# Decoder layer on one core: both V parts behind the scores of step 1, later feed-forward transposes and statistics, and one tile for B and C in the mixer

## The reference, cut to what matters

```python
# 1, mixer: u, B, C go through a causal convolution of 4 taps and a silu
zgate, u, Bc, Cc, dt = jnp.split(proj, [DIN, 2 * DIN, 2 * DIN + N_, 2 * DIN + 2 * N_], axis=-1)
Bc = Bc * jax.lax.rsqrt(jnp.sum(Bc * Bc, -1, keepdims=True) + 1e-06)
Cc = Cc * jax.lax.rsqrt(jnp.sum(Cc * Cc, -1, keepdims=True) + 1e-06)
z = (z + d * (Bu - A * y)) / (1.0 + d * d * A)      # per token, state of 16 per head
y = y + d * z                                        # out = y . C_t, then an MLP
# 2, attention: 16 heads of 64, one K and V for all heads, context of 375 tokens
attn = jax.nn.softmax(jnp.einsum('bhid,bjd->bhij', q, k) + mask[:, None, :, :], axis=-1)
out = jnp.einsum('bhij,bjd->bhid', attn, v)
out = out.transpose(0, 2, 1, 3).reshape(b, n, INNER) @ Wout + jax.nn.silu(gate) * val @ W2
# 3, feed-forward with both operands of the second product rounded to 8 bits
out = jnp.einsum('bsh,dh->bsd', hq, wq) + bq
```

## Time and profile before

| | us |
|---|---|
| three executions | 1742.54, 1746.35, 1747.15 |
| median | 1746.35 |
| the profiled execution | 1751.45 |
| its span, first to last instruction | 1749.6 |
| PE busy | 1604.0 (92%) |
| DVE busy | 1275.5 (73%) |
| ACT busy | 983.7 (56%) |
| POOL busy | 542.9 (31%) |

### The profile page before, as it was taken

One profiled execution on the slowest core, in us unless ns is written; L12 is line 12 of the kernel. 1 busy time (PEld: TensorE's weight loads), 2 busy tenths in 40 slices (PEclk: granted clock), 3 DMA queues, 4 the chain that ended last, 5 costly groups with the idle time before them and its releaser, 6 DMA issues.

```text
span 1749.6 us, 35590 instructions
## 1 busy us (share of the span) xinstructions
PE 1604.0 (92%) x13256; PEld 972.1 (56%) x13256; DVE 1275.5 (73%) x3633; ACT 983.7 (56%) x2326; POOL 542.9 (31%) x689
## 2 busy tenths in 40 slices
PE   4589999999999988799899899999999999999997
PEld 2356666667666744345455455455555455455476
DVE  6879889889895766666766766766766766856745
ACT  3434634635534255575665675675676666666652
POOL 3858768767776100120101101011011011011001
PEclk8688999999999988899999999999999999999999
DMA  4000010000001434443334334234334334333210
GB/s 140 11 12 12 11 33 12 22 24 21 22 2 41 156 88 102 139 101 89 76 87 107 71 86 108 72 80 102 86 78 98 90 75 100 87 82 91 63 28 22
DMA packets 177613, 119.24 MB, mean 68 GB/s; under 512 B 113856, under 2 KB 171136, under 8 KB 176544
## 3 DMA queue, kind: packets, MB, share of 16 engines
q1 hardware_dynamic: 176976, 116.50, 26.3%
q10 hardware_dynamic: 464, 0.46, 0.1%
HBM read 96.92 MB, written 7.42 MB: 60 GB/s over the span
## 4 chain that ended last, share of the span: by engine, by line
PE 70%; DVE 19%; issue 3%; DMA 3%; POOL 3%; ACT 2%; SPq 0%; DVEq 0%; POOLq 0%; ACTq 0%
PE ps L1633 18%; PE ps L1624 10%; PE ps L1588 8%; PE ps L1608 8%; PE ps L387 3%; PE ps L314 3%; PE ps L405 3%; DVE m_u L727 3%; PE ps L440 2%; PE ps L1693 2%; DVE m_rs L759 2%; PE ps L427 2%; PE ps L373 2%; POOL x_xs L1375 2%; DVE x_blk L1978 1%
## 5 line engine op out<-in xcount | busy, mean ns | idle before, releaser
L1964 DVE CUSTOM_DVE_ANT_0 x_pr<-ps,x_mk 128x375 f32<-128x375 f32 x448 | 226.3, 542 | 201.5 <-PE ps L1588 146.8
L1845 ACT ACTIVATE x_pr<-x_pr,x_rc 128x375 f32<-128x375 f32 x448 | 247.1, 599 | 148.8 <-DVE x_rc L1970 148.8
L1839 ACT ACTIVATE x_pr<-x_pr,x_mx 128x375 f32<-128x375 f32 x448 | 266.3, 595 | 111.4 <-DVE x_mx L1964 111.0
L1978 DVE STREAM_TRANSPOSE x_blk<-x_pr 128x384 f32<-128x384 f32 x448 | 232.0, 556 | 24.5 <-ACT x_pr L1845 24.5
L1544 POOL TENSOR_TENSOR x_cT<-x_cT,x_rb 128x375 f32<-128x375 f32 x64 | 57.1, 914 | 606.5 <-DMA x_rb<-context_roots 606.5
L1633 PE MATMUL ps<-x_xn,x_w 128*128 128x448 f32 x512 | 217.8, 564 | 5.3 <-DVE x_ff L2029 5.3
L1588 PE MATMUL ps<-x_kT,x_qT 64*128 64x375 f32 x896 | 178.7, 509 | 3.3 <-ACT x_kT L1888 3.3
L1608 PE MATMUL ps<-x_blk,x_va 32*64 32x224 f32 x6144 | 166.2, 358 | 12.9 <-DVE x_blk L1978 11.8
L1608 PEld LDWEIGHTS ps<-x_blk,x_va 32*64 32x64 f32 x6144 | 137.0, 133 | 55.0 <-issue 51.0
L1633 PEld LDWEIGHTS ps<-x_xn,x_w 128*128 128x128 f32 x512 | 95.7, 196 | 104.2 <-issue 82.6
L314 PE MATMUL ps<-m_xa,w_in 128*128 128x448 f32 x352 | 147.7, 567 | 6.2 <-ACT m_xa L532 6.2
(11 more groups left out here) (205 smaller groups left out, 2764.7 us busy)
## 6 DMA issues: line engine op xcount, KB each, us to landing
x_mk<-in_mask SPq DMA_DIRECT2D x224, 187.5 KB, 2.7
x_va<-x_vT SPq DMA_DIRECT2D x256, 48.0 KB, 2.1
x_cx<-in_context SPq DMA_DIRECT2D x32, 375.0 KB
x_cT<-in_context_turned SPq DMA_DIRECT2D x32, 375.0 KB, 3.7
x_rb<-context_roots SPq DMA_DIRECT2D x32, 187.5 KB, 4.5
m_Rd<-bc_roots SPq DMA_DIRECT2D x8, 448.0 KB, 3.6
x_mixed<-m_x SPq DMA_DIRECT2D x8, 448.0 KB, 3.8
X<-x_mixed SPq DMA_DIRECT2D x8, 448.0 KB, 4.1
```

Of the source, the lines that this page charges most:

```text
L1839: act.activation(pr[:, k, 0:J], pr[:, k, 0:J], ACT.Exp, scale=-1.0, bias=mx[:, k:k + 1], accum_out=sums[:, k:k + 1]).then_inc(h_e.sem, 1)
L1845: act.activation(pr[:, k + e, 0:J], pr[:, k + e, 0:J], ACT.Copy, scale=rc[:, k + e:k + e + 1]).then_inc(h_n.sem, 1)
L1964: dve.tensor_tensor_reduce(pr[:, k + e, 0:J], bank(SCORE_BANKS[p % NP] + e)[:, 0:J], mk[:, p % SLOT, :], -1.0, 3.0e38, ALU.add, ALU.min, m ...
L1978: dve.transpose(blocks[:, place_of(p), e, :, :].rearrange("p c x -> p (c x)"), pr[:, 2 * (p % SLOT) + e, :]).then_inc(h_t.sem, 1)
```

## The change

1. **Mixer, B and C in one tile.** NT is 10. Tile 1 holds B in partitions 0 to 63 and C in 64 to 127, each state four times. PE, ACT and DVE work on one tile `bc` (in buffer `r2`) in place of two, the squares are one instruction, and four DMAs for each group (`spread_bc`, 64 partitions x 448 elements each, 459 KB in all) copy `bc` to the two halves of both planes of `BCa`. `scale_bc` waits for them (`c_in`). ACT's first tap of `bc` waits for `right` of the group before (`a_R`), since `r2` is POOL's.
2. **V.** At remainder 0 PE now runs the scores of the next step, then both parts of `times_v`.
3. **Feed-forward transposes.** `ftoken` moves from step 17 to step 18.
4. **Statistics.** DVE runs `context_stats` between the X and Y pieces, and the statistics of the next tokens behind the Y pieces. The norm of `x_xs` at step 23 is halved: two sequences on POOL, two on DVE.
5. **Seats.** Queries 3 and 4 change seats (0 and 1 become 1 and 0), and the second `down` takes seat 2 in place of 1.

```diff
-NT = 3 + 2 * KI
+NT = 2 + 2 * KI
...
-    bsq = r1[0:64, 0, :, :].rearrange("p b s -> p (b s)")
+    bsq = r1[:, 0, :, :].rearrange("p b s -> p (b s)")
+    bc = r2[:, 0, :, :].rearrange("p b s -> p (b s)")
...
+        def spread_bc(i):
+
+            sp.wait_ge(a_si.sem, a_si.value(i, 1))
+            hold(sp, a_L, i - 1, 2)
+            for c in range(2):
+                for g in range(2):
+                    sp.dma_start(BCa[64 * g:64 * g + 64, c, :], bc[64 * c:64 * c + 64, :]).then_inc(c_in.sem, 16)
...
-        bc_tile(0, 1)
-        bc_tile(0, 2)
+        bc_tile(0)
...
-            if i + 1 < NG:
-                bc_tile(i + 1, 2)
             out_project(i, i + 1 < NG)
...
         def bc_parts(i):
-            hold(act, a_L, i - 1, 2)
-            tap(i, 0, 1, BCa[:, 0, :])
-            tap(i, 1, 2, BCa[:, 1, :])
+            hold(act, a_R, i - 1, a_R.per)
+            tap(i, 0, 1, bank(0), bc)
             hold(act, a_si, i - 1, a_si.per)
-            tanh_half(i, 0, BCa[:, 0, :], a_cv, 3)
-            tanh_half(i, 1, BCa[:, 1, :], a_cv, 6)
-            hold(act, a_R, i - 1, a_R.per)
-            for c in range(2):
-                act.wait_ge(a_si.sem, a_si.value(i, c + 1))
-                at = slice(32 * c, 32 * c + 32)
-                act.activation(bsq[at, :], BCa[at, c, :], ACT.Square).then_inc(a_bsq.sem, 1)
+            tanh_half(i, 0, bc, a_cv, 3)
+            act.wait_ge(a_si.sem, a_si.value(i, 1))
+            act.activation(bsq, bc, ACT.Square).then_inc(a_bsq.sem, 1)
...
         def bc_parts(i):
-            taps(i, 0, 1, BCa[:, 0, :])
-            taps(i, 1, 2, BCa[:, 1, :])
-            silu(i, 0, BCa[:, 0, :], BCa[:, 0, :])
-            silu(i, 1, BCa[:, 1, :], BCa[:, 1, :])
+            taps(i, 0, bank(0), bc)
+            silu(i, 0, bc, bc)
...
             roots_of = Rd[:, :, :, :].rearrange("p s b c -> p c b s")
+            dve.wait_ge(c_in.sem, c_in.value(i + 1, 0))
             dve.wait_ge(r_in.sem, r_in.value(i + 1, 0))
...
-SCORED = ((), (0,), (0, 1), (), (0, 1), (), (0, 1))
+SCORED = ((), (), (0, 1), (), (0, 1), (), (0, 1))
...
-        at[17, "X"].append(("ftoken", n))
+        at[18, "X"].append(("ftoken", n))
...
-SEAT = {"gate": (1,) * 8, "value": (3,) + (0,) * 7, "out": (1, 0), "kv": (2,) * 4, "query": (1, 1, 0, 0, 1, 0, 2, 3),
-        "back": (2, 3), "ftoken": (2, 3), "token": (2, 3), "down": (3, 1), "up": (1, 0) * 4}
+SEAT = {"gate": (1,) * 8, "value": (3,) + (0,) * 7, "out": (1, 0), "kv": (2,) * 4, "query": (1, 1, 0, 1, 0, 0, 2, 3),
+        "back": (2, 3), "ftoken": (2, 3), "token": (2, 3), "down": (3, 2), "up": (1, 0) * 4}
...
-            rooted(pool, 0, lambda b: token(X, it + 1, b), lambda b: xs[:, b, :], x_nm)
+            rooted(pool, 0, lambda b: token(X, it + 1, b), lambda b: xs[:, b, :], x_nm, range(GH))
...
-                if p % NP == V_AT[1] and (p >= NP or not first):
-                    i, at = back(it, p, NP)
-                    times_v(i, at // NP, 1)
...
                 if p % NP == V_AT[0] and (p >= NP or not first):
                     i, at = back(it, p, NP)
+                    scores(it, p + 1)
                     times_v(i, at // NP, 0)
+                    times_v(i, at // NP, 1)
...
-                if r == CONTEXT[0] and not (last and b >= 2):
-                    context_stats(it + (b + 2 > GB), (b + 2) % GB)
-                if p == TOKENS[0] and not last:
-                    tokens_norm(it, 0)
...
                 parts(it, p, "X", first, last)
+                if r == CONTEXT[0] and not (last and b >= 2):
+                    context_stats(it + (b + 2 > GB), (b + 2) % GB)
                 parts(it, p, "Y", first, last)
+                if p == TOKENS[0] and not last:
+                    tokens_norm(it, 0)
+                if p == TOKENS[2] and not last:
+                    dve.wait_ge(c_ln.sem, c_ln.value(it + 1, CROOT))
+                    filled(dve, it - 1, ("token", 1))
+                    rooted(dve, 0, lambda b: token(X, it + 1, b), lambda b: xs[:, b, :], x_nm, range(GH, GB))
```

More of the change, by code:

```diff
@@ L191, in mixer @@
     a_abs = count("a_abs", 3)
[L192 to L196, removed]
+    a_tap = count("a_tap", 1 + KI)
+    a_cv = count("a_cv", 3 * (1 + KI))
+    a_th = count("a_th", 1 + 2 * KI)
+    a_si = count("a_si", 1 + 2 * KI)
+    a_bsq = count("a_bsq", 1)
     a_bst = count("a_bst", 1)
     a_rr = count("a_rr", 3 + RSQRT)
+    c_in = count("m_cin", 4 * 16)
     r_out = count("m_rout", 16)
@@ L305, in turn_tokens @@
             else:
-                hold(pe, a_cv, i - 1, 3 * 4)
+                hold(pe, a_cv, i - 1, 3 * 3)
             for k in range(KD):
@@ L320, in dt_tile, with bc_tile @@
             in_tile(0, bank(6)[:, 0:T])
-        def bc_tile(i, n):
+        def bc_tile(i):
             hold(pe, b_mc, i - 1, 6)
-            in_tile(n, bank(n - 1)[:, 0:T])
+            in_tile(1, bank(0)[:, 0:T])
         def gate_tiles(i):
             hold(pe, b_mc, i - 1, 8)
[L328 to L332, removed]
+            for m in range(KI):
+                if m == 2:
+                    pe.wait_ge(a_cv.sem, a_cv.value(i, 3))
+                in_tile(2 + m, bank((2 + m) % 4)[:, 0:T])
+                if i == 0 and m == 1:
                     column_means(pe)
-                if n == 4:
+                if m == 1:
                     squared_sums(i)
@@ L338, in squared_sums @@
             hold(pe, b_yt, i - 1, b_yt.per)
-            pe.wait_ge(a_bsq.sem, a_bsq.value(i, 2))
+            pe.wait_ge(a_bsq.sem, a_bsq.value(i, 1))
             for b in range(GB):
-                last = pe.matmul(bank(5)[0:S, 2 * b:2 * b + 2], bsq[:, b * S:(b + 1) * S], heads_of, start=True, stop=True)
+                last = pe.matmul(bank(5)[0:S, 2 * b:2 * b + 2], bsq[:, b * S:(b + 1) * S], states_of, start=True, stop=True)
             last.then_inc(a_bst.sem, 1)
@@ L345, in u_tiles @@
             for m in range(KI):
-                pe.wait_ge(a_si.sem, a_si.value(i, 3 + m))
-                in_tile(3 + KI + m, bank((2 + m) % 4)[:, 0:T])
+                pe.wait_ge(a_si.sem, a_si.value(i, 2 + m))
+                in_tile(2 + KI + m, bank((2 + m) % 4)[:, 0:T])
                 if i == 0 and m == 1:
@@ L548, in step_relu, with tap @@
             act.activation(relu, bank(6)[:, 0:T], ACT.Relu, bias=dtb).then_inc(a_abs.sem, 1)
-        def tap(i, c, n, dst):
+        def tap(i, c, n, src, dst):
             act.wait_ge(a_proj.sem, a_proj.value(i, n + 1))
-            act.activation(dst, bank((n - 1) % 4)[:, 0:T], ACT.Identity, scale=cw[:, c, TAPS - 1:TAPS], bias=conv_b[:, c:c + 1]).then_inc(a_tap.sem, 1)
+            act.activation(dst, src[:, 0:T], ACT.Identity, scale=cw[:, c, TAPS - 1:TAPS], bias=conv_b[:, c:c + 1]).then_inc(a_tap.sem, 1)
         def tanh_half(i, m, src, ready, k):
@@ L746, in u_parts @@
                 if m < KI:
-                    taps(i, 2 + m, 3 + KI + m, ua[:, m, :])
+                    taps(i, 1 + m, bank((2 + m) % 4), ua[:, m, :])
                 if m >= 1:
-                    silu(i, 2 + KI + m - 1, ua[:, m - 1, :], ua[:, m - 1, :])
+                    silu(i, 1 + KI + m - 1, ua[:, m - 1, :], ua[:, m - 1, :])
         def softplus(i):
@@ L1370, in place_of, with rooted @@
         return tile_of(p) + AHEAD_BY * (p // NP % 2)
-    def rooted(eng, g, src, dst, done):
-        for b in range(GB):
+    def rooted(eng, g, src, dst, done, which=range(GB)):
+        for b in which:
             eng.tensor_scalar(dst(b), src(b), mv[0:S, GB * g + b, 0:1], rt[0:S, 1, g, b:b + 1], ALU.subtract, ALU.mult).then_inc(done.sem, 1)
@@ L1699, in group @@
                     parts(it, p, "X", first, last)
-                for ahead in SCORED[p % NP] if p or not first else (0,):
+                for ahead in SCORED[p % NP] if p > 1 or not first else (0,):
                     if not (last and p + ahead == STEPS):
```

32 lines of the change are left out of this document (17 added, 15 removed).

## The result

| | before | changed |
|---|---|---|
| median of four executions | 1746.75 us | 1693.53 us (1690.38 to 1694.46) |
| ratio of the times | | 0.9696, 95% interval 0.9675 to 0.9717 |
| profiled execution, its span | 1751.45, 1749.6 us | 1693.12, 1691.3 us |

The change takes 53 us, 3.0%. A second set of executions gave 0.9674 (0.9657 to 0.9691). The total is what was forecast; one term of it had the wrong sign, and two others were off the other way.

What follows compares the result with a forecast made beforehand. PE was taken as the bound, through its waits in attention and jointly with VectorE in the mixer. Terms 12 + 30 + 4 + 7 + 1.7 gave some 54 us, from 1746.35 to 1692 us; range 1678 to 1716 us.

Steps and rivals of the forecast that it cites:

- mixer: Mixer loop: PE loses one tile, 1.6 us in 7 groups plus 0.8 us in the opening; 12 us, bounds 4 and 14.
- groups 1 to 6, waits: Attention: shorter waits of PE save 5.0 us per group over six groups; 30 us, bounds 13 and 45.
- clock: Attention: half of the 6.9 us lost to lowered granted clock behind a wait returns; 4 us, between 0 and 6.9.
- group 0: First attention group: earlier scores bring step 14's maximum and kv 4.4 us earlier; 7 us with other steps, between 2 and 10.
- last group: Last attention group: only the moved transposes save time there; 1.7 us.
- Scores ahead of V: Attention groups: the next step's scores fill PE's waits for blocks ahead of V; 0.8 us per group.
- Transposes at step 18: Attention groups: moving them removes the 2.58 us wait, leaving a new 1.1 us wait for kv; 1.5 us per group.
- Statistics: Attention groups: statistics behind the pieces remove PE's 1.03 us wait ahead of the second "up" tile; 1.2 us per group.
- Half of the norm: Step 23: halving the `x_xs` norm, with roots 1.6 us earlier, cuts PE's 1.83 us wait; 1.7 us per group.
- Slower: Rival: 192 V matmuls in a row lower the clock to 1.2 GHz, 120 us cost, 1812 us; chance 0.03.
- Waits return: Rival: attention's new waits (kv, value, blocks, V's loads) grow; 32 us saved, 1714 us; chance 0.22.
- All waits go: Rival: all of attention's listed waits and the clock loss vanish; 77 us saved, 1669 us; chance 0.10.

Runs made afterwards that it cites:

- the mixer part alone: The kernel before with only the mixer's part of the change (B and C in one tile): 0.9938 (0.9915 to 0.9961), 10.8 us faster.
- attention's part alone: The kernel before with only attention's part of the change, the mixer as before: 0.9744 (0.9719 to 0.9769), 44.8 us faster.
- the kernel with POOL alone: The changed kernel with the whole norm of `x_xs` on POOL, VectorE's half removed: 0.9648 (0.9630 to 0.9666), period 128.36 us.

## Why the prediction was right, and where it was not

On the traces the sum stands so (forecast, measured between landmarks of the two traces: the last MLP product of the mixer, and the first V row of groups 1 and 7, less the 0.83 us of scores that now stand ahead of it):

| term | forecast | measured |
|---|---|---|
| mixer | 12 | 16.5 in this pair of traces; 10.8 timed alone |
| groups 1 to 6, waits | 30 | 27.6 |
| clock | 4 | 6.9 |
| group 0 | 7 | 4.7 |
| last group | 1.7 | 2.6 |
| sum | 54 | 58.3 |

- **Mixer.** The size holds. The reason was half right: PE alone holds the loop. The four DMAs cost nothing, as forecast: they start 14.4 us ahead of the row that needs them (16 us forecast), and 9 us of that is slack.
- **Scores ahead of V.** 1.0 us for 0.8 with the halved norm in place. This was the step undersized: with the norm left to POOL it brings 3.8 us, 0.3 us of it clock, since the roots of step 22, which the prediction saw come 1.6 us earlier, clear the `x_xs` wait by themselves.
- **Transposes at step 18.** The wait went, the two that the prediction put in its place came, at 0.62 us (1.1) for kv and 0.33 us for the value tile. The clock was under-counted: no dip is left, where half was expected.
- **Statistics.** 1.3 us for 1.2.
- **Half of the norm.** The step that failed. It was credited with 1.7 us, of which the earlier roots were 1.6: the same gain counted under the wrong cause. The row that contradicts it was on the page: POOL takes 4.83 us, and with 1.6 us more to take them in, a wait of 1.83 us is down to 0.2 us with no half moved. VectorE's half, 5 us behind the roots, could only be later. The kernel without this step has periods 1.2 us shorter, 0.6 us by the `x_xs` wait and 0.6 us by shorter stalls inside V. The overlap that the prediction weighed did not come: POOL's half ends at 1097.99 + 2.43 = 1100.42 us, VectorE's starts at 1102.98 us and takes 0.69 us.
- **Group 0.** The kv of step 14 came 5.6 us earlier against the mixer's end (127.9 us behind its last MLP product, 133.5 us before), as the mechanism said, more than its 4.4 us. But PE's wait went from 7.04 to 6.15 us only, not below 3:

```profile
694.26 2.87 PE L1696 MATMUL ps<-x_cT,x_wkv 128*128 128x375 f32 x4 [6.15 <-POOL x_cT L1547]
```

  PE too reaches that place 4.7 us earlier. Part of that is shorter waits ahead of it, and 1.7 us is V at step 14, whose first 96 matmuls took 4.21 us at a granted clock of 0.59 before, while all 192 take 4.80 us at 1.00 now. With the mixer part alone and the scores where they were the wait is 6.19 us, with attention's part alone 5.41 us, so the drop from 7.04 to 6.15 us by itself says little of the scores. A wait shrinks by the difference of two moves, and the prediction moved one end. Behind it the waits for the normed tokens and the queries are 3.6 us in place of 2.5 us, and 4.7 us remain of 7.
- **Rivals.** "Slower" by the clock did not come: the granted clock is 1.00 in all V rows of groups 1 to 6. Yet 192 small matmuls in a row do cost something, 7.5 us more of stalls less 28 x 0.18 = 5.0 us for the parts joined, by another mechanism than the one named. The row at the end of the last group, taken as proof against it, was one place in 32; at more than half of the others V in a row takes 4.72 us as well, and the loss sits in the few that meet a late transfer of code. "Waits return" fell, since each new wait stayed below 0.7 us. "All waits go" was 1669 us; the kernel with POOL alone, 0.9648 or some 1685 us, is a third of the way there from the forecast.

The median came out within 2 us of the forecast (1693.53 us for 1692 us), and in part by luck, through errors that cancel: too little for the scores and the clock, too much for the norm and group 0. The sum of 58.3 us in the table belongs to one pair of traces, of which the one before is 5 us above its median; between medians it is 53 us.

The fastest kernel of the study is the changed one with the norm of `x_xs` left to POOL: 0.9648 (0.9630 to 0.9666) and a period of 128.36 us, against 129.3 to 129.7 us.

## What to carry to other kernels

Where two edits in one change act on the same wait, work out each with the other in place: the gain belongs to whichever comes first, and the second may only add its cost. Before moving work to a faster engine, ask when that engine comes to it in its own order, not how long it takes. And a wait of a busy engine is a difference of two times, so move both of its ends before you price it.

## What the runs showed of the hardware

- PE stalls inside rows of 192 small matmuls, up to 1.6 us in a row, at the borders of 256 instructions of its code (behind matmul 153, 138 and 122 from group to group), with 105 code transfers of 16.4 KB. It went on 1.2 to 1.65 us after the end of the transfer in 70 of 72 stops of 0.2 us or more, and never sooner. Rows of 96 with 1.6 us of large matmuls between them lost at most 0.4 us in 56 rows.
- A single wait of 2.58 us is followed by stretches of 6 us with a granted clock of 0.72 to 0.85, part of them at 1.2 GHz in place of 2.4 GHz, in four groups of six before and in five of six with the transposes at step 17; a wait of 1.84 us is followed by one of 0.81 in one group of six. In kernels with no wait above 1.1 us it stayed at 1.00 through groups 1 to 6.
- Two V parts apart take 4.9 us, in a row 4.72 us.
